# Self-attention maxima by half of the queries, 10 slots ahead of the scores in place of 18, in a four-layer transformer on one core

## What is computed

```python
# layer 0 (16 heads of 16 features, 1024 queries x 1024 keys per sample)
x = x + gate * (self_attention(rope(q), rope(k), v, mask) @ Wo)   # "self attention"
x = x + gate * (attention(ln(x) @ Wq, ctx_k, ctx_v) @ Wco)        # cross attention, 77 keys
x = x + gate * mlp(ln(x))
# layer 1: cross attention of one head, three experts and a router, per token
# layer 2: the same three steps as layer 0, without rope and mask
# layer 3: x + (attention(ada_ln(x), ada_ln(ctx)) @ Wp)            # cross attention only
# every softmax: exp(s - max(s)) / sum(exp(s - max(s)))
```

## Time and profile before

| | us |
|---|---|
| median of 3 runs (3568.66 to 3597.33) | 3577.6 |
| time of the profiled execution | 3596.8 |
| its span, first to last instruction | 3594.9 |
| TensorE busy (94%) | 3371.6 |
| VectorE busy (51%) | 1829.8 |
| ScalarE busy (40%) | 1422.3 |
| GpSimd busy (7%) | 242.5 |

### The profile page before, as it was taken

One profiled execution on the slowest core, in us unless ns is written; L12 is line 12 of the kernel. 1 busy time (PEld: TensorE's weight loads), 2 busy tenths in 40 slices (PEclk: granted clock), 3 DMA queues, 4 the chain that ended last, 5 costly groups with the idle time before them and its releaser, 6 DMA issues.

```text
span 3594.9 us, 51053 instructions
## 1 busy us (share of the span) xinstructions
PE 3371.6 (94%) x20564; PEld 1877.9 (52%) x20564; DVE 1829.8 (51%) x3806; ACT 1422.3 (40%) x2591; POOL 242.5 (7%) x214
## 2 busy tenths in 40 slices
PE   4799999999889999998999999999999999999887
PEld 2555666756575666666433444534455444543464
DVE  4677565462412232324866765466655666553423
ACT  0144535444312222221355454554545546455332
POOL 0100010010100000001000010000100001000010
PEclk7899999989889999999899999999999999999797
DMA  5200000002000000001000000000000000000000
GB/s 170 79 1 6 8 20 4 20 6 93 16 22 0 1 1 1 0 1 54 1 1 1 1 7 4 1 24 7 7 4 16 10 7 7 4 16 15 1 1 12
DMA packets 57266, 58.14 MB, mean 16 GB/s; under 512 B 17728, under 2 KB 51249, under 8 KB 56765
## 3 DMA queue, kind: packets, MB, share of 16 engines
q1 hardware_dynamic: 57028, 54.79, 4.9%
HBM read 46.89 MB, written 7.89 MB: 15 GB/s over the span
## 4 chain that ended last, share of the span: by engine, by line
PE 90%; DVE 6%; ACT 2%; issue 1%; DMA 1%; SPq 0%; POOL 0%; DVEq 0%; ACTq 0%
PE ps L878 83%; PE ps L1042 3%; PE ps L1164 1%; PE ps L1022 1%; PE ps L1033 1%; ACT probs L1869 1%; DVE row_max_cross L1650 1%; ACT big L1827 1%; DVE bn_stats L1560 1%; DVE max_halves L1508 1%; PE ps L1142 0%; DMA big<-in_L_xcond_bss_kv 0%; DVE xn_tok L1573 0%; DVE row_max L1506 0%; DVE big L1656 0%
## 5 line engine op out<-in xcount | busy, mean ns | idle before, releaser
L1827 ACT ACTIVATE big<-ps 128x512 f32<-128x512 f32 x1280 | 687.3, 598 | 824.9 <-PE ps L878 824.2
L878 PE MATMUL ps<-big 32*128 32x512 f32 (+2 forms) x5760 | 950.5, 614 | 13.8 <-DVE row_max L1506 5.2
L1508 DVE TENSOR_REDUCE max_halves<-ps 128x1 f32<-128x512 f32 x1024 | 651.2, 684 | 376.6 <-PE ps L878 375.6
L878 PEld LDWEIGHTS ps<-big 32*128 32x128 f32 (+1 forms) x5760 | 392.9, 192 | 491.3 <-issue 385.7
L878 PE MATMUL ps<-big,probs 128*32 128x512 f32 (+1 forms) x2688 | 381.5, 610 | 15.0 <-ACT big L1827 8.7
L878 PE MATMUL ps<-weights_mlp,big 128*128 128x256 f32 (+1 forms) x1248 | 335.4, 421 | 2.5 <-ACT big L1881 2.5
L878 PEld LDWEIGHTS ps<-weights_mlp,big 128*128 128x128 f32 x1248 | 236.3, 191 | 85.8 <-issue 57.6
L1545 DVE TENSOR_TENSOR x_tok<-ps,x_tok 128x512 f32<-128x512 f32 x112 | 77.5, 692 | 338.5 <-PE ps L878 338.5
L878 PE MATMUL ps<-x_T,weights_mlp 128*128 128x256 f32 x1024 | 233.5, 388 | 3.3 <-ACT x_T L1844 3.2
L1869 ACT ACTIVATE probs<-ps 77x512 f32<-77x512 f32 x384 | 196.1, 592 | 83.5 <-PE ps L878 83.5
L878 PEld LDWEIGHTS ps<-x_T,weights_mlp 128*128 128x128 f32 x1024 | 197.1, 194 | 37.9 <-issue 5.6
(11 more groups left out here) (218 smaller groups left out, 3319.1 us busy)
## 6 DMA issues: line engine op xcount, KB each, us to landing
weights_mlp<-in_L_xcond_mlp_W SPq DMA_DIRECT2D x5, 1024.0 KB, 5.3
weights_mlp<-in_L_xcond_W_mlp SPq DMA_DIRECT2D x5, 1024.0 KB, 5.3
x_tok<-in_x SPq DMA_DIRECT2D x4, 1024.0 KB, 9.4
out_y<-x_tok SPq DMA_DIRECT2D x8, 512.0 KB, 2.9
big<-in_L_xcond_e_w SPq DMA_DIRECT2D x3, 1024.0 KB, 9.2
gates_biases<-mod_rows SPq DMA_DIRECT2D x20, 128.0 KB, 5.0
big<-in_L_xcond_adaLN_W SPq DMA_DIRECT2D x1, 2304.0 KB
kc_groups<-big SPq DMA_DIRECT2D x3, 616.0 KB, 4.0
```

What stands on the lines that cost most here:

```text
L878: return pe.matmul(out, lhsT, rhs, start=first, stop=last)
L1508: dve.tensor_reduce(NMP[:, e, j, s // NH, s % NH:s % NH + 1], PS[:, bank, :], AX.X, ALU.max, negate=True).then_inc(R.frees(key), 1)
L1827: act.activation(PB[:, score % 2, j, :], PS[:, R.bank(key), :], ACT.Exp, scale=SCALE).then_inc(R.frees(key), 1)
```

## The change

Maxima are made and turned for one block (half of the queries) at a time. `R.group` is gone; `R.lead` is `R.per` + 2, 10 slots in layer 2 and 4 in layer 0. A turn comes every 8 (2) slots, with one ring entry, 4 transposes and one write by VectorE; so does L1513, on half as much. `row_max` has 4 parts in place of 2, one for each half and parity of the group. `index` and `block` number the blocks; the argument `rows_first` that they read is empty in all three regions, so the order of the blocks is as before. `open_to` lets "qk" of the first half of the next sample's queries go as soon as the first half of the old has been read, one block earlier.

```diff
-        NM = sb("row_max", [P, 2, 160])
+        NM = sb("row_max", [P, 4, 160])
...
-                self.group = NH * self.per
-                self.total = NG * self.group
-                self.lead = self.group + 2
+                self.total = NG * NH * self.per
+                self.lead = self.per + 2
+                self.rows_first = rows_first
...
-                    return ... + [("nm", g, hf) for g in nms for hf in range(NH)]
+                    return ... + [("nm", q) for q in nms]
...
+            def index(self, b, g, qh):
+                return NH * NG * b + (qh * NG + g if b in self.rows_first else g * NH + qh)
+            def block(self, q):
+                b, u = divmod(q, NH * NG)
+                return (b, u % NG, u // NG) if b in self.rows_first else (b, u // NH, u % NH)
...
-            nms = ((base + ahead) // R.group - 1,) if 0 < ahead <= count and ahead % R.group == 0 else ()
+            nms = ((base + ahead) // R.per - 1,) if 0 < ahead <= count and ahead % R.per == 0 else ()
...
-                return (2.15 if tok[1] is not None else 0.0) + ... + 0.45 * len(tok[4]) + 0.9 * len(tok[5])
+                return (2.15 if tok[1] is not None else 0.0) + ... + 0.45 * len(tok[4]) + 0.45 * len(tok[5])
...
-                    return t >= (tok[1] - 1) * R.total + (2 * tok[2] + 2) * R.group
+                    return t >= (R.index(tok[1] - 1, 2 * tok[2] + 1, 1 if tok[3] else tok[4]) + 1) * R.per
...
-                if fill < NB * R.total and fill % (2 * R.group) == 0:
+                b, g, qh = R.block(fill // R.per)
+                if fill < NB * R.total and fill % R.per == 0 and qh == 0 and g % 2 == 0:
...
-                        pe.wait_ge(*R.freed(("nm", b * NG + g, qh)))
+                        pe.wait_ge(*R.freed(("nm", t // R.per)))
...
-                            pe.wait_ge(R.nm, gg + 1)
-                        for hf in range(NH):
-                            bank = take(("nm", gg, hf))
-                            for i in range(4):
-                                qt = 4 * hf + i
-                                last = pe.transpose(PS[:, bank, i * P:(i + 1) * P], NM[:, gg % 2, qt:qt + P], ident[:, :])
-                            done(last, ("nm", gg, hf))
+                            pe.wait_ge(R.nm, q + 1)
+                        b, g, qh = R.block(q)
+                        bank = take(("nm", q))
+                        for i in range(4):
+                            qt = 4 * qh + i
+                            last = pe.transpose(PS[:, bank, i * P:(i + 1) * P], NM[:, 2 * qh + g % 2, qt:qt + P], ident[:, :])
+                        done(last, ("nm", q))
...
-                        if (s, j) == (R.group - 1, 1):
+                        if (s, j) == (R.per - 1, 1):
                             dve.wait_ge(*R.freed(key))
-                            dve.tensor_tensor(dst, NMP[:, e, :, :, 0], NMP[:, e, :, :, 1], ALU.min).then_inc(R.nm, 1)
+                            dve.tensor_tensor(dst, NMP[:, e, :, 4 * qh:4 * qh + 4, 0], NMP[:, e, :, 4 * qh:4 * qh + 4, 1], ALU.min).then_inc(R.nm, 1)
```

More of the change, by code:

```diff
@@ L325, in entries @@
                     shown = [[("sc", score, j) for j in js] if score is not None else [] for js in ((0, 1), (2, 3))]
-                    return shown[0] + self.fills(fill, 0) + shown[1] + self.fills(fill, 1) + [("tail", q) for q in tails] + [("nm", g, hf) for g in nms for hf in range(NH)]
+                    return shown[0] + self.fills(fill, 0) + shown[1] + self.fills(fill, 1) + [("tail", q) for q in tails] + [("nm", q) for q in nms]
                 if kind in ("lnT", "oT"):
@@ L343, in fills @@
                     return []
-                gg, s = divmod(fill, self.group)
-                return [("max", gg, s, j) for j in ((2, 3), (0, 1))[half]]
+                return [("max",) + divmod(fill, self.per) + (j,) for j in ((2, 3), (0, 1))[half]]
+            def index(self, b, g, qh):
[3 more added lines that the diff above has]
+                return (b, u % NG, u // NG) if b in self.rows_first else (b, u // NH, u % NH)
             def at(self, slot):
-                b, t = divmod(slot, self.total)
-                g, r = divmod(t, self.group)
-                return (b, g) + divmod(r, self.per)
+                q, i = divmod(slot, self.per)
+                return self.block(q) + (i,)
             def buffer(self, x, b):
@@ L466, in cost @@
             if kind == "slot":
[L467 removed]
+                return (2.15 if tok[1] is not None else 0.0) + (1.05 if tok[2] is not None else 0.0) + 0.45 * len(tok[4]) + 0.45 * len(tok[5])
             if kind == "qk":
@@ L545, in open_to @@
                         return t > (tok[1] - 1) * R.total
-                    return t > (tok[1] - 1) * R.total + (2 * tok[2] + 2) * R.group
+                    return t > (R.index(tok[1] - 1, 2 * tok[2] + 1, 1) + 1) * R.per
                 if kind == "oT" and tok[1] == 0:
-                    return ("tail", 2 * NG * (tok[2] + 1) - NH + tok[3]) in ended and (tok[2] == 0 or all(k in ended for k in o_tokens(R, tok[2] - 1, tok[3])))
+                    return ("tail", R.index(tok[2], NG - 1, tok[3])) in ended and (tok[2] == 0 or all(k in ended for k in o_tokens(R, tok[2] - 1, tok[3])))
                 if kind == "cs":
@@ L571, in slot_ready @@
                         times.append(ended[k] + (4.5 if R.rope else 2.0))
-                if 1 <= t <= NB * R.total and (t - 1) % R.group == 0:
-                    b, g = divmod((t - 1) // R.group, NG)
+                if 1 <= t <= NB * R.total and (t - 1) % R.per == 0:
+                    b, g, qh = R.block((t - 1) // R.per)
                     if ("v", b, 0 if R.few else g // 2) not in ended:
@@ L577, in slot_ready @@
                 for q in tok[4]:
-                    b = q // (2 * NG)
-                    if b and ("oT", 0, b - 1, q % NH) not in ended:
+                    b, g, qh = R.block(q)
+                    if b and ("oT", 0, b - 1, qh) not in ended:
                         return None
@@ L956, in fill @@
                 def fill(key):
-                    _, gg, s, j = key
-                    b, g = divmod(gg, NG)
-                    if s == 0 and j == 2 and g % 2 == 0:
+                    _, n, s, j = key
+                    b, g, qh = R.block(n)
+                    if s == 0 and j == 2 and qh == 0 and g % 2 == 0:
                         for a in range(2):
@@ L1091, in region_pe @@
                         if x == 0:
-                            for q in range(hf, 2 * NG, NH):
-                                pe.wait_ge(*R.freed(("tail", 2 * NG * b + q)))
+                            for g in range(NG):
+                                pe.wait_ge(*R.freed(("tail", R.index(b, g, hf))))
                             turn_rows(tok, ATT, hf)
```

54 lines of the change are left out of this document (28 added, 26 removed).

## The result

The changed kernel takes 3556.0 us in the median of 22 runs (3551.3 to 3585.9), the kernel before 3577.5 in 22 runs beside it (3566.2 to 3604.1). The ratio is 0.9937 with a 95% interval of 0.9917 to 0.9956: 22 us less, between 16 and 30. The forecast was 14.6 us less. Its direction held and its range holds the time; its size lies just outside the interval, and 3556.0 lies between case A (3563) and case C (3553), nearer to C. The profiled execution took 3559.1 us, with a span of 3557.3 at a granted clock of 0.946; the one of before 3596.8 and 3594.9 at 0.937.

The account below looks back on a forecast made before the run. TensorE was taken to bound most stretches, VectorE's reductions the region starts. Gains of 24.0 us less 1.8 for fills and 7.6 for turns gave -14.6 us, median 3577.6 to 3563.0; range 3541 to 3592.

Parts of the forecast that it names:

- case A: Whole kernel: the forecast itself, 14.6 us less, median 3563 us; chance 0.46.
- case C: End of layer 2: a half-clock stretch goes too, 10 us more gained, 3553 us; chance 0.17.
- start of layer 2: Eight of 18 fills-only slots go, each 4 VectorE reductions of 0.601 us: 19.2 us gained, at least half.
- start of layer 0: Two of 6 fills-only slots go, 8 reductions of 0.601 us: 4.8 us gained.
- fills at the end: Fills return in the last 8 slots of layer 2 and two of layer 0: 1.8 us more, ends 0.3 and 4.6.
- 32 added turns: Splitting turns costs 0.47 us for ten groups, 0.13 for 22: 7.6 us more, ends 0 and 15.7.
- order and short distance elsewhere: Planner's new order of other tokens: counted as 0, with 12 us either way for one half-clock stretch.
- 4 x 3.89 + 3 x 0.49: Layer 0: four slots with one turn and two tails take 17.03 us, said to bear out the turn price.
- drain at a change of the array's tiling mode: TensorE at each of 32 added turns: a drain speaks against the change; trace agrees in sign, 0.13 us per interruption.
- B: Every added turn costs the full 0.49 us and end fills 4.6: only 3.7 us less, 3574 us; chance 0.20.
- D: Middle of kernel: planner's new order adds a half-clock stretch of 12 us, with dear turns, about 3586 us; chance 0.11.
- E: Added turns make TensorE wait for a pair of reductions each, 46 us in all, 3601 us; chance 0.06.

Follow-up runs that it names:

- turns_old_order: Against the kernel before: turns split block by block, old distances, planner's costs and queries condition kept as before; 3598.7 us, ratio 1.0044.
- turns_only: Against the kernel before: turns made block by block in both layers, fills kept at the old distances of 18 and 6 slots; 3587.3 us, ratio 1.0022.
- fills_to_the_end: turns_old_order with unused fills and reductions added in the last 18 slots of layer 2; 3590.4 us, ratio 1.0026 to the kernel before.
- l0_only: Against the kernel before: only layer 0 gets half-query units and a lead of 4, layer 2 left as before; 3576.0 us, ratio 0.9987.
- close: Against the kernel before: layer 0 unchanged, layer 2 with half-query units, lead 9, turn one slot ahead of its scores; 3587.9 us, ratio 1.0017.
- before_again: The kernel before, unchanged, profiled once more to see the spread between profiles; 3575.0 us.

## Why the prediction was right, and where its sizes were off

| term | forecast | found | from |
|---|---|---|---|
| start of layer 2 | -19.2 | -20.0 | table, the same in every kernel with the short distance to 0.3 us |
| start of layer 0 | -4.8 | -5.8 | table; the profiles differ by 0.4 |
| fills at the end | +1.8 | +2.5 | slots 238 to 249, 46.6 to 49.1 |
| 32 added turns | +7.6 | +6 | profiles of turns_old_order; by its runs 0.7 |
| order and short distance elsewhere | 0 | +6 | rest of L0's slots and slots 0 to 238, less the turns |
| clock outside the starts | 0 | -8 | below |

*Starts: right.* They are counts of reductions times 0.60 us. They came out 0.8 and 1.0 us larger than forecast. In layer 0 that surplus is the split turn's: turns_old_order and turns_only, which keep the old distance, start at 14.8 us in place of 15.6. That they were a sure gain rests on what the earlier trace rows showed: VectorE full. Layer 2's start had 41 us at half clock before and 20 after, and the time saved is still that of VectorE's reductions.

*Fills: right in kind.* 2.5 us lie between the 1.8 and the 4.6 given. In fills_to_the_end a lone slot paid 0.38 on average, where the forecast took 0.46.

*Turns: right in kind, too dear by 1.7 us or more.* One support of the sum was none: the 3.89 in "4 x 3.89 + 3 x 0.49" for layer 0 follows from the same 17.03 us; with the 3.85 of the earlier trace rows it would be 16.87. The slot with four transposes takes the forecast 4.34 us. That four of them stand in the first sample without other work beside them was right too: 2.0 us. But from the product of slot 0 to that of slot 64 the profiles give 272.7 us before and 274.0 after, 1.3 more: one slot in which an old turn met other work took 5.35 us and now takes 4.67. Splitting also relieves a slot that was too full; the sum had no term for that. The rule on the drain at a change of the array's tiling mode, in the Trainium skill, "TensorEngine Tiling (Array Packing)", section "Key Properties", holds in sign: the price found is about 0.18 us for each added interruption (5.9/32, by the profiles).

*Order: the term that failed.* "I take 0" was said of the planner's order, with 12 us either way for one stretch at half clock. The rest of layer 0 became 9.7 us longer with the clock taken out, of which 2.6 are turns. I had looked for waits in layer 2 and not for what a shorter distance does in layer 0, whose slots stand among cross attention throughout. Layer 0's part of the change is therefore worth nothing that can be measured (l0_only, 0.9987).

*The clock: not a term, though it was a rival.* The terms in microseconds add up to -20.0 - 5.8 + 2.5 + 9.7 + 2.0 = -11.6 (9.7 and 2.0 are after's rest of layer 0 and slots 0 to 238 against before's mean and 1472.9, half clock counted half, turns in them). The means of the runs are 3558.8 after and about 3579 before (in the experiments' batches), 20 less; against the batch of after itself (3582.3, for which there is no clock) it is 23.5. Of the rest, 8 to 12 us, the clock accounts for about 8: after ran 374 us at half clock in the mean, the kernel before 417 in the batch of 35 runs. Of these 43 us the starts are 28 (41 to 20 and 16 to 9), which saved nothing by the clock; the other 15, at half, are 7.5. So the total, off by 5 to 9 us, is hardly farther off than its largest parts: a term that should have stood at +6 and one at -8 nearly cancel. That is luck. The ends given for A, 3551 to 3577, are not those of its terms either: the full starts, 0.3 for fills and 0 for turns (-24.0 + 0.3) give 3554, and half of layer 2's start with the dearest fills and turns (-9.6 - 4.8 + 4.6 + 15.7) gives 3584.

*The rivals.* B fell: the turns cost 6 us at most, not 15.7. D is half right, as an order that costs, but at 3 to 6 us in layer 0 and by no stretch at half clock. E fell: waits ahead of turns are 3.9 us for 64. A wait that decides against a shorter distance was near, though, but behind the turn: with one slot less, close lost what layer 2 had won, about half of it by waits and half by the clock. C gave the nearer time (3553), but its mechanism is not borne out. The change doesn't remove the stretch: before_again, l0_only and turns_only lack it with the old distance in layer 2, and four kernels with the short distance have it. Nor does TensorE's share ahead of it decide (12.25 and 12.30 us of 20, 16.90 and 16.93, with both outcomes each time). Only with the slots full, in fills_to_the_end, was it absent where its partner had it, in one profile each, with 27 us less at half clock in the runs. The Trainium skill, "TensorE: Matmul & The Clock Gate", section "Part 1: The HAM clock gate", by which activity releases the throttled state, agrees with that pair (granted clock 0.51 without the fills, 1.00 with them); it doesn't tell before from before_again. What decides whether the stretch comes in a given run stays open, and so does why after has less half clock outside the starts.

## What to carry to other kernels

Where a run-up is bound by one engine that is full in its windows, count that engine's instructions: a gain of so many reductions times 0.60 us came out here to 1 us. Shorten a distance only down to the slowest step behind the hand-over: here the write of the maxima into the queries needed the second slot, and leaving it out cost all that layer 2 had won. The two profiles of the unchanged kernel differ by 38 us of half clock (453 and 415). In such a kernel, split each profile into stretches at fixed events and compare these with their half-clock time beside them; the totals of two profiles say little, and a change of 5 us can't be judged from them. Lay windows at the same event too before comparing how busy an engine was, and profile the unchanged kernel again before a stretch at half clock is put down to the change.

## What was not expected of the hardware

- The unchanged program gave 37.4 us with 24 at half clock for slots 249 to 255 in one profile, and 26.1 with none in the next, with the same instructions. Its runs had from 378 to 475 us at half clock over four batches.
- Adding work made a stretch shorter: 72 more fills and 72 more reductions, and slots 249 to 255 took 28.0 us in place of 37.5.
- Where VectorE was the bound, TensorE's half clock cost the reductions nothing: in the start of layer 2, with a clock of 0.61 to 0.63, one took 0.60 us; in the first sample of close, at a clock of 1.00, four take 2.48 us, which is no faster.
- The same 20 us of slots, with TensorE busy 12.25 and 12.30 us, were followed by 24 us at half clock in one profile of the unchanged kernel and by none in the other.
